# Attention loop: two score pairs moved to the front, products with the values ahead of a transposition, ScalarE reordered

## What is computed

```python
x = x + tanh(g_xattn[0]) * xattn(layernorm(x), ctx, ctx)   # 16 heads of 16, softmax(q k / 16) v, output projection
x = x + tanh(g_ffn[0]) * ffn(layernorm(x))                 # 256 -> 1024, relu squared, -> 256
x = x + tanh(g_xattn[1]) * align(ctx, layernorm(x))        # distances, dynamic time warping, backtrack, scatter-add
x = x + tanh(g_ffn[1]) * bitlinear_ffn(layernorm(x))
```

## Time and profile before

| | us |
|---|---|
| median of 3 runs (lowest, highest) | 2167.36 (2166.36, 2174.5) |
| the profiled execution, its own time | 2170.05 |
| its span, first to last instruction | 2168.3 |
| busy in the span: PE, DVE, ACT, POOL | 1573.3, 1575.6, 1025.7, 453.1 |
| mean granted clock of TensorE, share of full | 0.871 |

### The profile page before, as it was taken

How to read it: one execution, slowest core, us unless ns; L and a number is a source line. 1 busy time by engine, 2 the same in 40 slices (tenths; PEclk the granted TensorE clock), 3 DMA queues, 4 the chain that set the end, 5 groups by cost and what they waited for, 6 DMA issues and landing times. The chain is left out here.

```text
span 2168.3 us, 37941 instructions
## 1 busy us (share of the span) xinstructions
PE 1573.3 (73%) x10467; PEld 1100.0 (51%) x10467; DVE 1575.6 (73%) x5042; ACT 1025.7 (47%) x2104; POOL 453.1 (21%) x589
## 2 busy tenths in 40 slices
PE   3689999999999999999999986233320037777876
PEld 1357676776767767677776765000000014445443
DVE  6556666676666766667666653799989968999997
ACT  0155555545555454555555552233320016777675
POOL 3111221212112121121111211000000024454453
PEclk9799999999999999999999998555555558889898
DMA  2434334343343433334343310222200022122210
GB/s 70 123 106 128 99 107 123 92 128 99 111 115 93 125 103 111 112 97 121 104 121 96 96 49 21 48 62 60 55 15 0 0 86 63 61 72 74 74 54 30
DMA packets 321893, 179.20 MB, mean 83 GB/s; under 512 B 92769, under 2 KB 317169, under 8 KB 321794
## 3 DMA queue, kind: packets, MB, share of 16 engines
q1 hardware_dynamic: 321794, 178.07, 28.8%
HBM read 122.91 MB, written 50.33 MB: 80 GB/s over the span
## 5 line engine op out<-in xcount | busy, mean ns | idle before, releaser
L761 DVE TENSOR_REDUCE nmax<-s 128x2 f32<-128x512 f32 x512 | 325.9, 683 | 120.3 <-PE s L377 119.7
L576 ACT ACTIVATE pt<-s 128x512 f32<-128x512 f32 x512 | 277.4, 600 | 11.3 <-PE s L392 11.2
L460 PE MATMUL wb<-x2T,wfcT 128*128 128x256 f32 x1024 | 241.9, 379 | 1.4 <-issue 1.4
L849 POOL TENSOR_TENSOR r<-rl 128x512 f32<-128x512 f32 x128 | 133.0, 1039 | 455.6 <-ACT rl L598 453.9
L460 PEld LDWEIGHTS wb<-x2T,wfcT 128*128 128x128 f32 x1024 | 184.9, 190 | 23.0 <-issue 1.7
L392 PE MATMUL s<-qst,kst 128*128 128x256 bf16 x1024 | 170.8, 276 | 16.1 <-ACT pt L576 8.6
L377 PE MATMUL s<-kst,qst 96*128 96x256 bf16 x1024 | 163.8, 276 | 21.0 <-DVE nmax L761 13.6
L404 PE MATMUL oacc<-pt,vw 128*32 128x256 f32 x2048 | 137.1, 385 | 45.9 <-ACT pt L576 45.9
L1362 PE MATMUL ph<-w1T,xqT 128*128 128x512 bf16 x384 | 119.0, 475 | 36.9 <-ACT xqT L1424 36.9
L1145 PE MATMUL gate<-diag,one 128*128 128x512 f16 x35 | 21.3, 608 | 171.3 <-DVE left L1220 171.3
L598 ACT ACTIVATE rl<-wb 128x512 f32<-128x512 f32 x128 | 76.3, 596 | 145.0 <-PE wb L460 145.0
(11 more groups left out here) (240 smaller groups left out, 3735.6 us busy)
## 6 DMA issues: line engine op xcount, KB each, us to landing
kst<-k_parts_dram SPq DMA_DIRECT2D x384, 64.0 KB, 2.6
qst<-q_parts_dram SPq DMA_DIRECT2D x384, 64.0 KB, 2.4
k_parts_dram<-kp SPq DMA_DIRECT2D x32, 384.0 KB, 4.7
q_parts_dram<-qp SPq DMA_DIRECT2D x32, 384.0 KB, 3.1
xin<-in_x_dram SPq DMA_DIRECT2D x32, 256.0 KB, 2.8
cT<-in_ctx_T_dram SPq DMA_DIRECT2D x32, 256.0 KB, 2.7
xres<-in_x_dram SPq DMA_DIRECT2D x32, 256.0 KB, 2.9
cin<-in_ctx_dram SPq DMA_DIRECT2D x32, 256.0 KB, 4.3
```

The source lines that it names most:

```text
L460: last = pe.matmul(B_FC[k][:, j, :], wfcT[:, c, f * P:f * P + P], x2T[:, c, :], start=(c == 0), stop=(c == C - 1))
L576: act.activation(pt[h % (2 * HPG)][:], s2[h % 2][:], ACT.Exp).then_inc(e["expd"], 1)
L761: v.tensor_reduce(nmax[:, T * h:T * h + T], s1[h % 2][:], AX.X, ALU.max, negate=True)\
L849: pool.tensor_tensor(r2[:], rl[:, k % 2], rl[:, k % 2], ALU.mult)\
```

## The change

On TensorE, `scores2(i, 0, 2)` moves up to between `scores1(s, 2, 4)` and `proj(y, 1)`, and `scores2(i, 2, 4)` to between `scores1(s, 4, 6)` and `out_proj(z)`. `values(i, 0)` and `scores2(i, 4, 6)` come ahead of `values_proj(s)`; `scores1(s, 6, 8)`, `scores2(i, 6, 8)` and `values(i, 1)` come ahead of `turn_y(y)`. On ScalarE the exponentials and group copies are reordered to match. VectorE's order stays. Three pairs of semaphores become one each (`aa_half` and `aa_sum`; `recip` and the chain of the norms; `quant_p` and `quant_f` in the set-up), with the waits on the same events.

```diff
@@ TensorE, iteration
                 if there(s):
                     scores1(s, 2, 4)
+                if there(i):
+                    scores2(i, 0, 2)
                 if there(y):
                     proj(y, 1)
                 if there(s):
                     scores1(s, 4, 6)
+                if there(i):
+                    scores2(i, 2, 4)
                 if there(z):
                     out_proj(z)
                 if there(a):
                     queries(a)
                 if there(i):
-                    scores2(i, 0, 2)
+                    values(i, 0)
+                    scores2(i, 4, 6)
                 if there(s):
                     values_proj(s)
-                if there(i):
-                    scores2(i, 2, 4)
-                    values(i, 0)
-                    scores2(i, 4, 6)
+                    scores1(s, 6, 8)
+                if there(i):
+                    scores2(i, 6, 8)
+                    values(i, 1)
                 if there(y):
                     turn_y(y)
                 if there(z):
                     turn_xh2(z)
-                if there(s):
-                    scores1(s, 6, 8)
-                if there(i):
-                    scores2(i, 6, 8)
                 if there(y):
                     products(y)
                     row_norms(y)
                 if there(i):
-                    values(i, 1)
                     scores2(i, 8, 10)
@@ ScalarE, iteration
                 if there(z):
                     ctx_squares(z)
+                if there(i):
+                    exps(i, 0, 4)
                 if there(a):
                     qh_copy(a)
                 if there(i):
-                    exps(i, 0, 2)
+                    copy_group(i, 0)
+                    exps(i, 4, 6)
+                if there(a):
+                    middle_part(a, "q_rem", qr, qp, "q_parts_mid")
                 if there(s):
                     values_copy(s)
                 if there(i):
-                    exps(i, 2, 4)
-                if there(a):
-                    middle_part(a, "q_rem", qr, qp, "q_parts_mid")
-                if there(i):
-                    copy_group(i, 0)
-                    exps(i, 4, 6)
+                    exps(i, 6, 8)
+                    copy_group(i, 1)
                 if there(y):
                     yT_copy(y)
                 if there(z):
                     xh2_copy(z)
-                if there(i):
-                    exps(i, 6, 8)
                 if there(y):
                     bb_copy(y)
                 if there(i):
-                    copy_group(i, 1)
                     exps(i, 8, 10)
@@ VectorE, normalise
-                v.reciprocal(rs[:], o[:, :, :, DH]).then_inc(e["recip"], 1)
-                w("recip", 2 * b.n + half + 1, 2 * NB), w("on_t", b.n)
+                nc_.link(v.reciprocal(rs[:], o[:, :, :, DH]))
+                w("on_t", b.n)
@@ ScalarE, ctx_squares (and the waits for aa_sum count T per batch)
                 for t in range(T):
-                    if t:
-                        act.wait_ge(e["aa_half"], b.n + 1)
-                    else:
-                        w("aa_sum", b.n)
-                    ins = act.activation(junk[:], cin[b.p][:, t, :], ACT.Square, accum_out=aa[b.p][:, t:t + 1])
-                    ins.then_inc(e["aa_half"] if t == 0 else e["aa_sum"], 1)
+                    w("aa_sum", T * b.n + t, T * NB)
+                    act.activation(junk[:], cin[b.p][:, t, :], ACT.Square, accum_out=aa[b.p][:, t:t + 1])\
+                        .then_inc(e["aa_sum"], 1)
```

More of the change, by code:

```diff
@@ L173, in attention_phase @@
                  "xT_cp", "qh_cp", "kh_cp", "vw_cp", "onT_cp", "x2T_cp", "relu", "expd", "o_cp", "yT_cp", "bb_cp",
-                 "dist", "aa_half", "aa_sum",
-                 "ln1", "q_rem", "k_rem", "maxed", "max_split", "recip", "normed", "x1_res", "ln2", "x2_res", "ln3",
+                 "dist", "aa_sum",
+                 "ln1", "q_rem", "k_rem", "maxed", "max_split", "normed", "x1_res", "ln2", "x2_res", "ln3",
                  "d_part",
@@ L228, in load_ctx @@
             def load_ctx(b):
-                w("aa_sum", b.n - 1)
+                w("aa_sum", T * (b.n - 1), T * NB)
                 sp.dma_start(cin[b.p][:], c_d[b.n].rearrange(tok, p=P)).then_inc(c_in[b.p], 16)
@@ L607, in ctx_squares @@
                 for t in range(T):
-                    if t:
-                        act.wait_ge(e["aa_half"], b.n + 1)
-                    else:
-                        w("aa_sum", b.n)
-                    ins = act.activation(junk[:], cin[b.p][:, t, :], ACT.Square, accum_out=aa[b.p][:, t:t + 1])
-                    ins.then_inc(e["aa_half"] if t == 0 else e["aa_sum"], 1)
+                    w("aa_sum", T * b.n + t, T * NB)
+                    act.activation(junk[:], cin[b.p][:, t, :], ACT.Square, accum_out=aa[b.p][:, t:t + 1])\
+                        .then_inc(e["aa_sum"], 1)
             def distance(b):
                 w("d_part", b.n + 1), w("d_out", 16 * T * b.n, 16 * T * NB)
-                w("aa_sum", b.n + 1)
+                w("aa_sum", T * (b.n + 1), T * NB)
                 for t in range(T):
@@ L884, in setup_weights @@
         ps = [ctx.enter_context(nc.psum_tensor(f"su{r}", [P, 4 * P], F32)) for r in range(6)]
-        small, fc_in, pr_in, straight, consts, quant_p, quant_f, turned, copied, tanhd, vch = (sem(n) for n in (
-            "w_small", "wfc_in", "wpr_in", "w_straight", "consts", "quant_p", "quant_f", "turned", "copied", "tanhd",
+        small, fc_in, pr_in, straight, consts, quant, turned, copied, tanhd, vch = (sem(n) for n in (
+            "w_small", "wfc_in", "wpr_in", "w_straight", "consts", "quant", "turned", "copied", "tanhd",
             "w_chain"))
@@ L934, in _ @@
                 ch.link(v.tensor_copy(sclb[:, a, :], scl[:, FT + a:FT + a + 1].broadcast_to((P, P))))
-            v.sem_inc(quant_p, 1)
+            v.sem_inc(quant, 1)
             v.wait_ge(fc_in, 16)
             quantise_rows(v, ch, wfc, scl[:, 0:FT], rsc[:, 0:FT], FT, D)
-            v.sem_inc(quant_f, 1)
+            v.sem_inc(quant, 1)
             v.wait_ge(turned, 1)
@@ L962, in _ @@
             pe.wait_ge(consts, 1)
-            pe.wait_ge(quant_p, 1)
+            pe.wait_ge(quant, 1)
             for k in range(4):
@@ L972, in _ @@
                 last.then_inc(turned, 1)
-            pe.wait_ge(quant_f, 1)
+            pe.wait_ge(quant, 2)
             for a in range(C):
```

## The result

The changed kernel takes 2257.86 us, median of 4 runs (2256.22 to 2261.74), against 2167.43 before (now the median of four runs, three of which gave the 2167.36 above). The ratio is 1.0419, with a 95% interval of 1.0396 to 1.0441: slower by 90 us. The prediction was 2268, in a range of 2212 to 2300.

A forecast was written before the change was run, and what follows sets the result against it. TensorE, busy 94% of the attention loop, was taken to set the pace. 1.87 us of wait plus 1.8 of clock in 28 iterations, less 2, gave +101 on 2170.05; the median was put at 2268 us, range 2212 to 2300.

The forecast's parts named there:

- qr and the chain: VectorE's remainder qr ends a gapless chain begun after `proj(y, 1)`; start and end would come 0.47 us later.
- E: The moment VectorE's remainder qr ends, 719.64 in the trace of before; predicted to move to 720.11.
- The removed wait: TensorE's 1.37 us wait before the values of group 0 goes, with 0.26 us of heads 6 and 7.
- The new wait: TensorE waits 3.7 us before the values of group 1; ScalarE's `middle_part`, ahead of their exponentials, waits for qr.
- What is late next: `fc(z, 0)`, waiting for VectorE's `distance_part`, starts 1.87 us later and lengthens the period by that; bounds 1.4 and 2.2.
- The clock: TensorE falls to half clock around its 3.7 us wait, costing 1.8 us per iteration; bounds 0 and 3.0.
- short stretch: TensorE at half clock for 3.4 us, 0.7 of it inside ScalarE's copy; charged 1.35 us.
- long one: TensorE at half clock for 6.8 us, some 1.5 before the wait ends and 0.7 in the copy; charged 2.3 us.
- The sum: 1.87 + 1.8 = 3.67 us in 28 full attention iterations, 103 us, and about -2 at the ends: +101 us.
- the rival with the clock at 1.00: The attention loop has the wait for `middle_part` but no lowered stretches: 2217 us, 2202 to 2227; chance 0.20.
- The clock that holds: Same wait for `middle_part`, TensorE staying at full clock: +50 us, 2217 us; chance 0.20.
- The faster side: VectorE's qr comes early enough, before 718.24, so removed TensorE waits count: down to 2137 us; chance 0.05.

The follow-up runs named there:

- seven matmuls: The changed kernel with 7 fp32 matmuls without use on TensorE ahead of the values of group 1 in full iterations: 2216.23 us, ratio 1.0223.
- the run with only the front part: The changed kernel with TensorE from `turn_y` on and ScalarE from yT on in the order of before: 2174.75 us, ratio 1.0026.

## Why the prediction was right, step by step

*qr and the chain.* Predicted: E moves by 0.47. Measured from the transpose of xhat: 719.64 - 701.71 = 17.93 before (701.71 is its start in the trace of before), 718.60 - 700.22 = 18.38 after, +0.45. The start of the chain moves the same (8.20 to 8.65). The reason given, heads 0 and 1 ahead of `proj(y, 1)`, is not the only one: with them behind it, qr still ends at 18.41, held up by the output projection.

*The removed wait.* As predicted, the values of group 0 wait for nothing.

*The new wait.* Predicted 3.7 us on TensorE and about 3 on ScalarE; 3.68 and 3.10 in the rows. That it is the cause is shown twice, once from each end of the link (middle part later, qr earlier): both bring back more than the whole loss.

*What is late next.* `fc(z, 0)` directly behind `distance_part`: 729.57 and 729.66. The period without the clock's part was predicted 1.87 us longer; with the seven matmuls it is 1.81 longer.

*The clock.* The step that needed a choice. The wait of 3.7 us was followed by a stretch at 0.50, 1.2 GHz, as after the 3.11 and the 5.51 of the earlier trace rows, in each of the 26 iterations. The rule that I had cited from the Trainium skill, in "TensorE: Matmul & The Clock Gate", section "HAM oscillation — how this bites in real kernels", agrees with that. I had charged 1.8 us per iteration, chosen between 1.35 for a short stretch and 2.3 for a long one, by halves of stretches of the earlier trace rows; it is 1.57 to 1.61. The two prices were close (1.1 to 1.3 and 2.2 to 2.5 measured); what no row of before could tell was the mixture, 19 short and 7 long, and the 1.8 was a choice and not a result. The values at half clock, for which I had only bounds of 0 and 1.0 on top, take 0.87 more in the iteration shown. The loop's mean clock is 0.95, where I had said near 0.9. That figure did not follow from my own stretches: 3.4 to 6.8 us lowered in a period of 42.2 make a mean of 0.96 to 0.92.

*The sum.* I had 3.67 us in each of 28 full iterations. The 28 periods that end in these iterations took 1077.3 us before and 1170.9 after, 3.34 each, so 9 us less than predicted. The period of 41.98 overstates it a little: two of its six have a long stretch, and the first and last unrolled iterations lose only 3.0 to 3.1. The other three periods between the transposes gave back 5 us, and outside the transposes another 2.6 came back, where I had allowed 2 in all. So the span grew by 86.1 us and not by 101. The profiled execution of after, 2256.22 us, is thus 15 under the 2271 that I had for it. The median is only 10 under my 2268, because the profiled execution of after lies under its median and that of before over its own; that part is luck. One bound was also added up wrongly: 28 x 1.4 - 2 = 37 gives 2205 us for the lower end of the rival with the clock at 1.00, not 2202; nothing else rests on it.

*The rivals.* The clock that holds is what the run with seven matmuls made: 2216.23 us, against 2217 worked out. The faster side would have needed qr 1.87 us earlier; with qr some 4 us earlier the kernel was indeed faster than before, by 27 us (30 worked out for that case); its period is 0.83 shorter, where I had 1.1. So the mechanism of that rival was right, and its condition is not met in the change.

## What to carry to other kernels

In queues that are written by hand, put an instruction that waits for a late result behind everything that doesn't need it: what is lost isn't that instruction's wait but that of all behind it, here the exponentials of two heads and through them TensorE. When a change moves consumers forward, ask where their producers stand in the other queues, and move these in the same change; the same new order loses 90 us with qr late and gains 27 with qr early. A wait of TensorE that recurs in each iteration may have to be priced twice, once as time and once for the clock behind it: here one of 3.68 us made the period 1.8 us longer, with the removed waits taken off, and the clock behind it another 1.6, while one of 1.37 left the clock at 1.00. Filling the wait with work without use is a quick way to tell the two apart.

## What the runs showed of the hardware that I had not expected

The clock can also fall after waits that are each shorter than one that is harmless: in the kernel before, 1.37 us is the longest wait of an iteration and the loop's clock is 1.00, but in the run with only the front part, waits of 1.05 and 0.68 us with one group of transposes between were followed by a slow group in about every third iteration, and the loop's mean clock was 0.99. So one can't judge by the longest wait alone, nor by the waits of one iteration: in the two iterations between, the same waits left the clock at 1.00. What decides between them was not tried.

```profile
150.00:1240.00 1090.00, 1027.01 (x7379) 784.83 (x7377) 706.86 (x1739) 599.83 (x1271) 211.44 (x198) 0.99 0.38 108
```

And the phases behind attention, which no run reordered, took between 810.1 us (after) and 814.6 us (front part only), counted from the start of the last `distance_part` to the end of the span; in before it is 810.6. Of the 7.5 us between the spans of the run with only the front part and of the kernel before, 4.0 come from there. Most of the rest comes from the last iterations of attention, where TensorE in that run has one longer wait and half clock behind it:

```profile
1289.41 1.11 PE L312 MATMUL wb<-ident,yn 128*128 128x128 f32 x4 [3.59 <-DVE yn L695]
```

The last transpose of the maxima stands at 1273.1 in that run and at 1272.8 in before. Why the phases behind attention differ was not tried, and stays open; it means that a few us in the median of a kernel need not come from the part that was changed.
